# A Mamba scan: the diagonals of B are written by DMA into DRAM and loaded, in place of being built by engines

## The chip, the core and the metric

The kernel runs on one core of a Trainium2 chip. Its engines are TensorE (PE: matrix products and transposes), VectorE (DVE), ScalarE (ACT), GpSimd (POOL) and SyncE (SP, which here only issues transfers); 16 DMA engines move data between DRAM and the on-chip memory SBUF. Time is the device time of one execution in microseconds (us), from the first to the last instruction with what lies around it.

## The reference

Input x has the shape (4, 32, 32, 384). A group norm, then a visual Mamba block whose result is added to x, then another group norm and a mixture of experts, added too. The work of this case is the selective scan in the Mamba block, over sequences of L = 1024 positions, 192 channels, 16 states, for 4 directions of each of 4 images:

```
dA = exp(d_t[..., None] * As)
h  = h * dA + (d_t * u_t)[..., None] * B_t[:, :, None, :]
y  = einsum('bkcn,bkn->bkc', h, C_t)
```

d_t, B_t and C_t come from the projection x_proj. All is float32.

## The kernel before

Three parts: `head` (norm, projections, convolution; its results xd hold the rows of dt, B and C in DRAM), `scan`, and `tail` (output norm, gate, projection and experts). The change is in `scan`, and a few lines of it in `head`.

**Units and steps.** A unit is one direction of one image: 16 units, u = 0 to 15, `unit_of` gives image b, orientation o and side s. A unit has 24 steps i: 8 pairs of states n (NP), by 3 groups g of 64 channels (CG). In one step, 128 partitions hold 2 states of 64 channels, and the row has 1024 positions. Each step runs through four engines:

- PE, `spread_b` (L1002): 64 products of 64 by 64 make the input term (dt u) B in PSUM (`pb`, two buffers). A product has dt u of 64 positions by 64 channels on one side, and on the other a 64 x 64 diagonal matrix with the values of B of one state at those positions. So a position's B scales it and the product turns positions into the free dimension at the same time.
- ACT, `decay` (L1084): exp(dt A), two steps ahead.
- DVE, `step_h` (L1158): the scan itself, out of `a` and `pb` into `h`, of which there are three triples of steps (TRIPLES).
- POOL, `times_c` (L1193): h times C, twice a triple; `crow`, the row of C broadcast to the partitions, is loaded by SP (L943) with three buffers.
- PE, `add_y` (L1041): sums over states in PSUM, seven steps (LAG) behind the first.

A scan of the first step of a triple waits until `add_y` has emptied the triple of three before. `spread_b` of a step waits for the scan of two steps before, since `pb` has two buffers.

**The diagonals.** `dd`, 32 KB x 128 partitions or 4 MB, holds all of them for one unit: 16 states by 8 blocks by 64 columns; upper and lower 64 partitions hold the diagonals of positions in the two halves r of a block. It is made in four pieces of 4 states. Pieces 1 and 3 are built by POOL (`build_d`, L199), one product of a broadcast of `bt` and a mask each; pieces 0 and 2 by ACT (`build_rows`, L284), 32 small instructions each that are dealt out over 12 steps. Piece p of the next unit may be written when `spread_b` has passed step 6(p + 1) of this one (`b_row`). `bt`, B with the positions on partitions, is made by the chunk "BT": PE transposes rows of xd (L223), ACT copies them (L262).

**Chunks.** The next unit is prepared by small pieces of PE work, each put behind the two PE parts of a certain step: Z (4 chunks, steps 0 to 3), BT (step 4), UT (4 chunks, steps 5 to 8, only when the next unit is even), DUP (4 chunks, steps 16 to 19). All share one PSUM bank, `pm`, and ACT empties it after each. ACT and DVE compute the softplus between steps 4 and 15.

**The SP queue.** SP goes through the units and the pairs n in order: crow; at n = 0 the rows of the next unit (L119, L120) and in odd units u or y (L127, L133; L975 in the last); at n = 7 the doublings of dt (L209). It waits in order, so that what stands behind a wait is late too. When an image is done, y is copied out by ACT (L1089, L1090) and stored (L949, L952).

The order on each engine is that in which the code issues; nothing reorders it.

Of the kernel before, what the change touches and what calls it, by code (L numbers as in the profile page):

```python
# [11 lines left out]
P = 128  # L12
BATCH = 4
HW = 32
L = HW * HW
# [5 lines left out]
N = 16  # L21
# [27 lines left out]
LAST_U = UNITS - 1  # L49
KINDS = (2, 0, 1)  # L50
# [25 lines left out]
def chunks_of(u):  # L76

    order = [("Z", ch) for ch in range(4)] + [("BT", 0)]
    if u % 2 == 0:
        order += [("UT", ch) for ch in range(4)]  # L80
    return order + [("DUP", i) for i in range(4)]
# [33 lines left out]
def load_rows(sp, d, keep, shared, u):  # L115

    b, o, s = unit_of(u)
    rows = keep["rows"]
    sp.dma_start(rows[0:R], d["xd"][b, o, s * PR:s * PR + R]).then_inc(shared["rows_in"], 16)  # L119
    sp.dma_start(rows[PR:PR + N], d["xd"][b, o, 2 * PR + s * N:2 * PR + (s + 1) * N]).then_inc(shared["rows_in"], 16)  # L120
# [26 lines left out]
class Units:  # L147

    def __init__(self, nc, ctx, keep, ys, shared):
# [16 lines left out]
        self.bt = sb("bt", [P, 2, N, BLK])  # L166
# [23 lines left out]
        self.b_row = sem("b_row")  # L190
        self.dup_in = [sem(f"dup_in{g}") for g in range(CG)]

    def build_d(self, eng, tt, u, piece):

        eng.wait_ge(self.chunk_taken, CHUNK[u, "BT", 0] + 1)
        need(eng, self.b_row, STEPS * (u - 1) + 6 * (piece + 1) if u else 0)
        rows_n = slice(4 * piece, 4 * piece + 4)
        shape = [P, 4 * BLK, HALF]
        tt(self.dd[:, rows_n].rearrange("p n k j -> p (n k) j"),  # L199
           self.bt[:, u % 2, rows_n].rearrange("p n k -> p (n k)").unsqueeze(2).broadcast_to(shape),  # L200
           self.keep["mask"][:].unsqueeze(1).broadcast_to(shape), ALU.mult).then_inc(self.d_odd if piece % 2 else self.d_even, 1)
# [9 lines left out]
    def chunk(self, pe, u, what, i):  # L211
# [4 lines left out]
        if what == "Z":  # L216
            pe.wait_ge(self.shared["rows_in"], 16 * 2 * (u + 1))
# [23 lines left out]
    def take_chunk(self, act, u, what, i):  # L241
# [7 lines left out]
        if what == "BT":  # L249
            need(act, self.d_even, 2 * (u - 1))  # L250
            need(act, self.d_odd, 2 * (u - 1))
            dst = self.bt[:, u % 2].rearrange("p n k -> p k n")
            src = pm[:, 0:BLK * N].rearrange("p (k n) -> p k n", k=BLK)
# [23 lines left out]
    def build_rows(self, act, u, piece, lo, hi):  # L277

        if lo == 0:
            act.wait_ge(self.chunk_taken, CHUNK[u, "BT", 0] + 1)  # L280
            need(act, self.b_row, STEPS * (u - 1) + 6 * (piece + 1) if u else 0)
        for at in range(lo, min(hi, 4 * BLK)):
            n, blk = 4 * piece + at // BLK, at % BLK
            row = self.nc.scalar.activation(self.dd[:, n, blk], self.keep["mask"][:], ACT.Identity,  # L284
                                            scale=self.bt[:, u % 2, n, blk:blk + 1])
        if hi >= 4 * BLK:
            row.then_inc(self.d_even, 1)
# [111 lines left out]
def head(nc, d, keep, keep_from, ys, m, shared):  # L399
# [5 lines left out]
    with ExitStack() as ctx:  # L405
# [271 lines left out]
        def _(act):  # L677
# [112 lines left out]
            m.build_rows(act, 0, 2, 0, 2 * BLK)  # L790
# [91 lines left out]
        @block.gpsimd  # L882
        def _(pool):
            nc.gpsimd.memset(xpad[:], 0.0).then_inc(borders, 1)
            pool.wait_ge(shared["kept_in"], 16 * len(KEPT))
            pool.wait_ge(turned, NC * BATCH)
            for piece in range(2):
                m.build_d(pool, nc.gpsimd.tensor_tensor, 0, piece)


def scan(nc, d, keep, ys, m, norm, shared):

    with ExitStack() as ctx:
# [42 lines left out]
        def _(sp):  # L936
# [50 lines left out]
        def _(pe):  # L987
            def spread_b(u, i):
# [76 lines left out]
        def _(act):  # L1065
# [29 lines left out]
            for u in range(UNITS):  # L1095
                b, o, s = unit_of(u)
                for i in range(STEPS):
# [3 lines left out]
                    if u + 1 < UNITS:  # L1101
# [85 lines left out]
        def _(pool):  # L1187
# [550 lines left out]
def bass_vision_mamba_moe(nc, x, eye, win, wx, gavg, conv_p, ones, wdt, apar, dpar, mask, wout, ln_g, ln_b, wr, rb, w1, b1, w2, b2, spread, eyeb, out):  # L1738
    def scratch(name, shape, dt=F32):
# [8 lines left out]
        xd=scratch("xd", (BATCH, 2, P, L)), u=scratch("u", (PAIRS, KIND, P, L)), ub=scratch("ub", (PAIRS, 2, KIND, P, L)), y=scratch("y", (PAIRS, KIND, P, L)),  # L1748
# [111 lines left out]
```

## Time and profile before

| | us |
|---|---|
| Times of three runs | 1640.47, 1642.54, 1648.41 |
| Median | 1642.54 |
| Profiled execution | 1650.07 |
| Its span | 1648.3 |

| Engine | busy us | share |
|---|---|---|
| PE | 1349.6 | 82% |
| DVE | 1229.3 | 75% |
| POOL | 1026.4 | 62% |
| ACT | 1014.8 | 62% |

SP's queue (q1) moved 146.83 MB in 73,200 packets, 30.3% of the 16 DMA engines' time. Another 240 packets, 3.93 MB, are instructions on q8. The scan runs from 187 us or so to 1342 us, a unit in about 71 us; head and tail take the rest. Busy shares are means over parts with different limits, so a unit has to be read by itself.

### The profile page before, as it was taken

The numbers are of one execution on the slowest core, as the hardware profiler recorded it, in microseconds if no ns is written. First come the engines' busy times: TensorE is split into PE (matmuls) and PEld (weight loads), VectorE is DVE, ScalarE is ACT, GpSimd is POOL, SyncE is SP. The second block draws the span as 40 slices with busy tenths as digits, with TensorE's granted clock in tenths as the row PEclk, the third lists the DMA queues.
The fourth block names the chain that finished last, engine by engine and source line by source line (L and its number), as shares of the span: only waits on it lengthen the run. The fifth ranks groups of instructions, "written<-read, shape, count | busy, mean of one in ns | idle before, by whom it ended". The sixth has DMA issues, their size and how long they took to land. (4 is left out here: it accounts for less than half of the span.)

```text
span 1648.3 us, 66375 instructions
## 1 busy us (share of the span) xinstructions
PE 1349.6 (82%) x30408; PEld 824.1 (50%) x30408; DVE 1229.3 (75%) x1025; ACT 1014.8 (62%) x1916; POOL 1026.4 (62%) x294
## 2 busy tenths in 40 slices
PE   6997779687886979788697878869787867879998
PEld 5734546444554545455454545545454534436554
DVE  4984298979798897989889798888979884733220
ACT  2558578766777877677787767777776640402222
POOL 0002189879797988889798889979888870000000
PEclk8998689999999999999999999999999997879999
DMA  9334324323232432323343232324323325101101
GB/s 324 125 148 185 112 65 107 96 67 96 54 90 73 110 91 72 96 68 90 74 109 86 77 91 73 90 73 109 86 77 81 97 81 196 39 0 39 39 29 48
DMA packets 73478, 151.08 MB, mean 92 GB/s; under 512 B 33238, under 2 KB 41942, under 8 KB 72816
## 3 DMA queue, kind: packets, MB, share of 16 engines
q1 hardware_dynamic: 73200, 146.83, 30.3%
q8 instruction: 240, 3.93, 1.0%
q14 instruction: 38, 0.31, 0.1%
HBM read 101.72 MB, written 32.51 MB: 81 GB/s over the span
## 5 line engine op out<-in xcount | busy, mean ns | idle before, releaser
L1193 POOL TENSOR_TENSOR s_h<-s_h,s_crow 128x2048 f32<-128x2048 f32 (+1 forms) x256 | 880.2, 3469 | 198.0 <-DVE s_h L1158 197.9
L1158 DVE TENSOR_TENSOR_SCAN s_h<-s_a,s_pb 128x1024 f32<-128x1024 f32 x384 | 864.2, 2277 | 183.6 <-PE s_py L1041 78.5
L1002 PE MATMUL s_pb<-k_area,m_dtut 64*64 64x64 f32 x24576 | 470.2, 224 | 194.2 <-DVE s_h L1158 162.8
L1002 PEld LDWEIGHTS s_pb<-k_area,m_dtut 64*64 64x64 f32 x24576 | 424.1, 138 | 384.6 <-DVE s_h L1158 230.1
L1041 PE MATMUL s_py<-s_h,k_eye 64*64 64x512 f32 x3072 | 417.8, 603 | 20.4 <-ACT y_y L1090 15.6
L284 ACT ACTIVATE k_area<-k_mask,m_bt 128x64 f32<-128x64 f32 x992 | 273.9, 337 | 0.0
L1084 ACT ACTIVATE s_a<-y_y,m_aneg 128x1024 f32<-128x1024 f32 x192 | 218.6, 1139 | 39.9 <-DVE s_h L1158 39.8
L1084 ACT ACTIVATE s_a<-m_dup,m_aneg 128x1024 f32<-128x1024 f32 x192 | 219.5, 1143 | 29.7 <-DVE s_h L1158 29.7
L199 POOL TENSOR_TENSOR k_area<-m_bt,k_mask 128x2048 f32<-128x2048 f32 x33 | 145.8, 4419 | 126.1 <-ACT m_bt L262 126.1
L1041 PEld LDWEIGHTS s_py<-s_h,k_eye 64*64 64x64 f32 x3072 | 90.1, 137 | 33.3 <-ACT y_y L1090 16.0
L262 ACT COPY y_y<-m_pm 128x384 f32<-128x384 f32 (+1 forms) x96 | 49.2, 513 | 91.8 <-PE m_pm L219 79.2
L1070 ACT ACTIVATE m_pm<-y_y 128x512 f32<-128x512 f32 x45 | 26.8, 596 | 98.5 <-DVE y_y L1141 98.5
L219 PEld LDWEIGHTS m_pm<-k_wdt,k_rows 25*128 25x128 f32 x256 | 42.4, 196 | 56.9 <-issue 56.5
L1473 PE MATMUL t_small<-k_w,k_area 128*128 128x384 f32 x192 | 70.4, 504 | 0.0
L1538 ACT COPY t_out<-t_small 128x384 f32<-128x384 f32 x32 | 15.3, 479 | 88.4 <-PE t_small L1476 88.4
L1448 PE MATMUL t_big<-t_xn,k_w 128*128 128x512 f32 x144 | 67.9, 623 | 0.0
L219 PE MATMUL m_pm<-k_wdt,k_rows 25*128 25x192 f32 x256 | 62.5, 366 | 6.5 <-DMA k_rows<-scratch_xd 6.5
L805 DVE SCALAR_TENSOR_TENSOR h_acc<-h_xpad,h_conv_p,h_acc 128x1024 f32<-128x1024 f32 x48 | 61.7, 1285 | 1.6
L238 PEld LDWEIGHTS m_pm<-k_eye,y_y 64*64 64x64 f32 (+1 forms) x512 | 33.6, 123 | 52.9 <-issue 49.9
L1659 DVE TENSOR_TENSOR k_area<-k_area,t_big 128x1024 f32<-128x1024 f32 x12 | 14.3, 1219 | 50.6 <-PE t_big L1462 50.4
L1473 PEld LDWEIGHTS t_small<-k_w,k_area 128*128 128x128 f32 x192 | 37.0, 197 | 18.5 <-issue 1.9
L238 PE MATMUL m_pm<-k_eye,y_y 64*64 64x64 f32 (+1 forms) x512 | 42.9, 224 | 2.7 <-ACT y_y L262 2.7
(189 smaller groups left out, 1233.5 us busy)
## 6 DMA issues: line engine op xcount, KB each, us to landing
s_crow<-scratch_xd SPq DMA_DIRECT2D x256, 256.0 KB, 4.0
k_area<-in_x_dram SPq DMA_DIRECT2D x4, 1536.0 KB, 8.0
scratch_xt<-y_y SPq DMA_DIRECT2D x4, 1536.0 KB, 10.2
y_y<-y_y SPq DMA_DIRECT2D x24, 256.0 KB, 3.6
m_dup<-m_dup SPq DMA_DIRECT2D x24, 256.0 KB, 3.2
out_dram<-t_out SPq DMA_DIRECT2D x32, 192.0 KB, 1.9
k_area<-scratch_xt SPq DMA_DIRECT2D x3, 1536.0 KB, 6.9
scratch_xd<-h_dbl SPq DMA_DIRECT2D x8, 512.0 KB, 2.6
```

Of the source, the lines that this page charges most:

```text
L199: tt(self.dd[:, rows_n].rearrange("p n k j -> p (n k) j"), self.bt[:, u % 2, rows_n].rearrange("p n k -> p (n k)").unsqueeze(2).broadcast_ ...
L219: mm = pe.matmul(pm[:, x * DI:(x + 1) * DI], tokens(rows[0:R + 1], 2 * i + x), self.keep["wdt"][:, o + 2 * s], start=True, stop=True)
L238: mm = pe.transpose(pm[0:chans.stop - chans.start, blk::BLK], self.dt_of[here, blk, chans], eye[here, here])
L284: row = self.nc.scalar.activation(self.dd[:, n, blk], self.keep["mask"][:], ACT.Identity, scale=self.bt[:, u % 2, n, blk:blk + 1])
L805: eng.scalar_tensor_tensor(out, view, w, out, ALU.mult, ALU.add).then_inc(convolved[kind], 1)
L1002: mm = pe.matmul(pb[par * HALF:(par + 1) * HALF, step % 2, r * BANK + blk:(r + 1) * BANK:BLK], dtut[here, u % 2, blk, g * HALF:(g + 1) * H ...
L1041: mm = pe.matmul(dst, eye[here, here], src, start=opens, stop=closes)
L1084: nc.scalar.activation(a[:, step % RING], dup[u % 2][:, g], ACT.Exp, scale=aneg[:, col:col + 1]).then_inc(a_ready, 1)
L1158: nc.vector.tensor_tensor_scan(h[:, step % (TRIPLES * CG), f], a[:, step % RING, f], pb[:, step % 2, f], 0.0, ALU.mult, ALU.add).then_inc( ...
L1193: nc.gpsimd.tensor_tensor(here, here, c.unsqueeze(1).broadcast_to([P, groups.stop - groups.start, L]), ALU.mult).then_inc(hc_ready, 1)
L1448: mm = pe.matmul(big_of("F1", b, j)[:, q], w1[:, c, j * P:(j + 1) * P], xn[:, b % 2, c, q], start=(c == 0), stop=(c == NC - 1))
L1473: pe.matmul(ps, hid[:, j, tok], w2[:, j], start=False, stop=False, skip_group_check=True)
```

## The change

From unit 1 on no engine builds diagonals. A scratch tensor `dd` in DRAM, four pieces of 128 x 2048 floats, gets the diagonals of unit 0 by `store_d`, zeros included. For each later unit `write_diagonal` overwrites the 64 places of each diagonal, straight from the rows of B in xd, also in DRAM: two DMAs a piece, one for each half r, with 32 diagonals of 64 elements; neighbours in the destination lie 2,049 elements apart. `load_d` then brings the piece, 1 MB, into SBUF. All on SP's queue: for unit u + 1 the writes of pieces 0 to 2 at n = 2, 4, 6 and the loads at n = 3, 5, 7; piece 3 at n = 0 and 1 of its own unit. PE waits for the load's semaphore (`d_in`).

The chunk BT, the load of its rows, and `build_d` and `build_rows` stay for unit 0 alone; `bt` has one buffer. The rows of the next unit wait for its chunk Z 3 in place of BT.

The core of the diff:

```diff
-    order = [("Z", ch) for ch in range(4)] + [("BT", 0)]
+    order = [("Z", ch) for ch in range(4)]
+    if u == 0:
+        order += [("BT", 0)]
...
+    def write_diagonal(self, sp, d, u, piece):
+
+        b, o, s = unit_of(u)
+        sp.wait_ge(self.d_stored[piece] if u == 1 else self.d_in[piece], 16 * max(u - 1, 1))
+        there = d["dd"][piece]
+        first = 2 * PR + s * N + 4 * piece
+        rows = d["xd"][b, o, first:first + 4].rearrange("n (k r j) -> r (n k) j", r=2, k=BLK)
+        for r in range(2):
+            diagonal = bass.AP(tensor=there.tensor, offset=there.offset + r * HALF * QUARTER, ap=[[HALF, 4 * BLK], [QUARTER + 1, HALF]])
+            sp.dma_start(diagonal, rows[r], allow_slow_non_contiguous=True).then_inc(self.d_written[piece], 16)
+
+    def load_d(self, sp, d, u, piece):
+
+        sp.wait_ge(self.d_written[piece], 32 * u)
+        sp.wait_ge(self.b_row, STEPS * (u - 1) + 6 * (piece + 1))
+        sp.dma_start(self.quarter(piece), d["dd"][piece]).then_inc(self.d_in[piece], 16)
+
+    def store_d(self, sp, d, piece):
+
+        sp.wait_ge(self.d_odd if piece % 2 else self.d_even, piece // 2 + 1)
+        sp.dma_start(d["dd"][piece], self.quarter(piece)).then_inc(self.d_stored[piece], 16)
...
                     if n == 0 and u + 1 < UNITS:
-                        sp.wait_ge(chunk_done, CHUNK[u, "BT", 0] + 1)
+                        sp.wait_ge(chunk_done, CHUNK[u, "Z", 3] + 1)
                         load_rows(sp, d, keep, shared, u + 1)
...
+                    if u == 0 and n < 4:
+                        m.store_d(sp, d, n)
+                    if n in (2, 4, 6) and u + 1 < UNITS:
+                        m.write_diagonal(sp, d, u + 1, (n - 2) // 2)
+                    if n in (3, 5, 7) and u + 1 < UNITS:
+                        m.load_d(sp, d, u + 1, (n - 3) // 2)
+                    if n == 0 and u:
+                        m.write_diagonal(sp, d, u, 3)
+                    if n == 1 and u:
+                        m.load_d(sp, d, u, 3)
...
-                    pe.wait_ge(d_odd if piece % 2 else d_even, 2 * u + piece // 2 + 1)
+                    if u == 0:
+                        pe.wait_ge(d_odd if piece % 2 else d_even, piece // 2 + 1)
+                    else:
+                        pe.wait_ge(m.d_in[piece], 16 * u)
...
-                        if 6 <= i < 18:
-                            m.build_rows(act, u + 1, 0, share(i - 6), share(i - 5))
-                        if i >= 18:
-                            m.build_rows(act, u + 1, 2, share(i - 18), share(i - 17))
-                    if i < 6:
-                        m.build_rows(act, u, 2, share(i + 6), share(i + 7))
+                    if u == 0 and i < 6:
+                        m.build_rows(act, 2, share(i + 6), share(i + 7))
...
-                    if n == 1:
-                        m.build_d(pool, nc.gpsimd.tensor_tensor, u, 3)
-                    if n == 4 and u + 1 < UNITS:
-                        m.build_d(pool, nc.gpsimd.tensor_tensor, u + 1, 1)
+                    if u == 0 and n == 1:
+                        m.build_d(pool, nc.gpsimd.tensor_tensor, 3)
```

## Rows read from the trace of the kernel before

**Rows 1.** Waits, whole run: engine, line, releaser; us in total, times, longest.

```profile
DVE s_h L1158 <- PE s_py L1041: 78.5, 72, 4.6
...
DVE s_h L1158 <- PE s_pb L1002: 63.2, 43, 6.1
...
PE s_pb L1002 <- issue: 25.4, 31, 3.6
...
PE s_py L1041 <- ACT y_y L1090: 15.6, 3, 5.2
```

**Rows 2.** Groups by line: count, busy us, mean ns; idle before, releasers.

```profile
L1041 PE MATMUL s_py<-s_h,k_eye 64*64 64x512 f32 x3072 | 417.8, 603 | 20.4 <-ACT y_y L1090 15.6 <-POOL s_h L1193 2.3 <-issue 1.2
L284 ACT ACTIVATE k_area<-k_mask,m_bt 128x64 f32<-128x64 f32 x992 | 273.9, 337 | 0.0
...
L199 POOL TENSOR_TENSOR k_area<-m_bt,k_mask 128x2048 f32<-128x2048 f32 x33 | 145.8, 4419 | 126.1 <-ACT m_bt L262 126.1
```

**Rows 3.** Windows: thirds of one unit; busy us (instructions), clock, DMA share, GB/s.

```profile
556.00:581.00 25.00, 25.00 (x706) 16.96 (x706) 20.18 (x9) 21.55 (x43) 23.09 (x8) 1.00 0.29 77
581.00:605.00 24.00, 15.65 (x536) 8.89 (x528) 22.54 (x19) 15.06 (x32) 18.80 (x6) 1.00 0.29 80
605.00:627.00 22.00, 19.00 (x603) 12.32 (x604) 20.43 (x11) 17.17 (x36) 22.00 (x7) 1.00 0.40 109
```

**Rows 4.** Timeline around BT: start us, us, what; in brackets idle before.

```profile
567.25 0.67 PE L223 MATMUL m_pm<-k_eye,k_rows 16*128 16x16 f32 x8
...
567.85 1.16 PE L1002 MATMUL s_pb<-k_area,m_dtut 64*64 64x64 f32 x64
...
570.90 1.16 PE L1002 MATMUL s_pb<-k_area,m_dtut 64*64 64x64 f32 x64
...
573.09 4.46 DVE L1158 TENSOR_TENSOR_SCAN s_h<-s_a,s_pb 128x1024 f32<-128x1024 f32 x2 [1.73 <-PE s_py L1041]
```

**Rows 5.** Timeline of DVE in a unit without UT, steps 3 to 6.

```profile
781.33 6.67 DVE L1158 TENSOR_TENSOR_SCAN s_h<-s_a,s_pb 128x1024 f32<-128x1024 f32 x3 [1.47 <-PE s_py L1041]
788.46 4.47 DVE L1158 TENSOR_TENSOR_SCAN s_h<-s_a,s_pb 128x1024 f32<-128x1024 f32 x2 [0.46 <-PE s_py L1041]
```

**Rows 6.** Timeline where ACT takes y away.

```profile
499.96 0.81 ACT L284 ACTIVATE k_area<-k_mask,m_bt 128x64 f32<-128x64 f32 x3
...
503.08 0.57 ACT L284 ACTIVATE k_area<-k_mask,m_bt 128x64 f32<-128x64 f32 x2
...
505.08 1.88 PE L1041 MATMUL s_py<-s_h,k_eye 64*64 64x512 f32 x8 [5.19 <-ACT y_y L1090]
```

**Rows 7.** DMA in 507.6:508.9, 1276:1279 and 546:617: packets, or queue with share.

```profile
DMA packets 1683, 0.13 MB, mean 98 GB/s; under 512 B 1678, under 2 KB 1678, under 8 KB 1683
...
DMA packets 240, 0.96 MB, mean 321 GB/s; under 512 B 5, under 2 KB 5, under 8 KB 240
...
q1 hardware_dynamic: 3076, 6.65, 34.2%
```

**Rows 8.** DMA in 401:406 and 406:407; PE's timeline at three stops.

```profile
q1 hardware_dynamic: 483, 1.24, 90.2%
...
DMA packets 875, 0.23 MB, mean 233 GB/s; under 512 B 874, under 2 KB 874, under 8 KB 874
...
q8 instruction: 1, 0.02, 7.5%
...
408.75 0.62 PE L1002 MATMUL s_pb<-k_area,m_dtut 64*64 64x64 f32 x26 [2.68 <-issue]
...
701.10 0.74 PE L1002 MATMUL s_pb<-k_area,m_dtut 64*64 64x64 f32 x34 [1.89 <-issue]
...
1282.33 0.97 PE L1002 MATMUL s_pb<-k_area,m_dtut 64*64 64x64 f32 x50 [3.58 <-issue]
```

**Rows 9.** DMA issues (KB, us to landing), then SP's timeline.

```profile
scratch_y<-y_y SPq DMA_DIRECT2D x8, 128.0 KB, 6.1
...
546.88 1.10 SPq L943 DMA_DIRECT2D s_crow<-scratch_xd  x2
```

More of the change, by code:

```diff
@@ L49 @@
 LAST_U = UNITS - 1
+QUARTER = 4 * BLK * HALF
 KINDS = (2, 0, 1)
@@ L119, in load_rows @@
     sp.dma_start(rows[0:R], d["xd"][b, o, s * PR:s * PR + R]).then_inc(shared["rows_in"], 16)
-    sp.dma_start(rows[PR:PR + N], d["xd"][b, o, 2 * PR + s * N:2 * PR + (s + 1) * N]).then_inc(shared["rows_in"], 16)
+    if u == 0:
+        sp.dma_start(rows[PR:PR + N], d["xd"][b, o, 2 * PR + s * N:2 * PR + (s + 1) * N]).then_inc(shared["rows_in"], 16)
 def load_u(sp, d, keep, shared, b, what):
@@ L165, in __init__ @@
         self.dtut = sb("dtut", [P, 2, BLK, DI])
-        self.bt = sb("bt", [P, 2, N, BLK])
+        self.bt = sb("bt", [P, N, BLK])
         self.amin = sb("amin", [P, UNITS // BATCH * STEPS])
@@ L190, in __init__, with build_d @@
         self.b_row = sem("b_row")
+        self.d_in = [sem(f"d_in{piece}") for piece in range(4)]
+        self.d_stored = [sem(f"d_stored{piece}") for piece in range(4)]
+        self.d_written = [sem(f"d_written{piece}") for piece in range(4)]
         self.dup_in = [sem(f"dup_in{g}") for g in range(CG)]
-    def build_d(self, eng, tt, u, piece):
-        eng.wait_ge(self.chunk_taken, CHUNK[u, "BT", 0] + 1)
-        need(eng, self.b_row, STEPS * (u - 1) + 6 * (piece + 1) if u else 0)
+    def build_d(self, eng, tt, piece):
+        eng.wait_ge(self.chunk_taken, CHUNK[0, "BT", 0] + 1)
         rows_n = slice(4 * piece, 4 * piece + 4)
@@ L199, in build_d @@
         tt(self.dd[:, rows_n].rearrange("p n k j -> p (n k) j"),
-           self.bt[:, u % 2, rows_n].rearrange("p n k -> p (n k)").unsqueeze(2).broadcast_to(shape),
+           self.bt[:, rows_n].rearrange("p n k -> p (n k)").unsqueeze(2).broadcast_to(shape),
            self.keep["mask"][:].unsqueeze(1).broadcast_to(shape), ALU.mult).then_inc(self.d_odd if piece % 2 else self.d_even, 1)
@@ L216, in chunk @@
         if what == "Z":
-            pe.wait_ge(self.shared["rows_in"], 16 * 2 * (u + 1))
+            pe.wait_ge(self.shared["rows_in"], 16 * (u + 2))
             for x in range(2):
@@ L249, in take_chunk @@
         if what == "BT":
-            need(act, self.d_even, 2 * (u - 1))
-            need(act, self.d_odd, 2 * (u - 1))
-            dst = self.bt[:, u % 2].rearrange("p n k -> p k n")
+            dst = self.bt[:].rearrange("p n k -> p k n")
             src = pm[:, 0:BLK * N].rearrange("p (k n) -> p k n", k=BLK)
@@ L275, in exponent, with quarter, build_rows @@
             nc.scalar.activation(self.wz, ez, ACT.Identity, bias=1.0).then_inc(self.w_ready, 1)
-    def build_rows(self, act, u, piece, lo, hi):
+    def write_diagonal(self, sp, d, u, piece):
[14 more added lines that the diff above has]
+        sp.dma_start(d["dd"][piece], self.quarter(piece)).then_inc(self.d_stored[piece], 16)
+    def quarter(self, piece):
+        return self.keep["area"][:].rearrange("p a l -> p (a l)")[:, piece * QUARTER:(piece + 1) * QUARTER]
+    def build_rows(self, act, piece, lo, hi):
         if lo == 0:
-            act.wait_ge(self.chunk_taken, CHUNK[u, "BT", 0] + 1)
-            need(act, self.b_row, STEPS * (u - 1) + 6 * (piece + 1) if u else 0)
+            act.wait_ge(self.chunk_taken, CHUNK[0, "BT", 0] + 1)
         for at in range(lo, min(hi, 4 * BLK)):
@@ L284, in build_rows @@
             row = self.nc.scalar.activation(self.dd[:, n, blk], self.keep["mask"][:], ACT.Identity,
-                                            scale=self.bt[:, u % 2, n, blk:blk + 1])
+                                            scale=self.bt[:, n, blk:blk + 1])
         if hi >= 4 * BLK:
@@ L789, in _ @@
             act.wait_ge(turned, NC * BATCH)
-            m.build_rows(act, 0, 2, 0, 2 * BLK)
+            m.build_rows(act, 2, 0, 2 * BLK)
         def convolve(eng, pair, kind, taps=range(9)):
@@ L887, in _ @@
             for piece in range(2):
-                m.build_d(pool, nc.gpsimd.tensor_tensor, 0, piece)
+                m.build_d(pool, nc.gpsimd.tensor_tensor, piece)
 def scan(nc, d, keep, ys, m, norm, shared):
@@ L995, in spread_b @@
                     piece = i // 6
-                    pe.wait_ge(d_odd if piece % 2 else d_even, 2 * u + piece // 2 + 1)
+                    if u == 0:
+                        pe.wait_ge(d_odd if piece % 2 else d_even, piece // 2 + 1)
+                    else:
+                        pe.wait_ge(m.d_in[piece], 16 * u)
                 need(pe, h_ready, step - 1)
@@ L1747, in bass_vision_mamba_moe @@
         xt=scratch("xt", (BATCH, NC, P, L)), sz=scratch("sz", (PAIRS, P, TT, 2 * DI)),
-        xd=scratch("xd", (BATCH, 2, P, L)), u=scratch("u", (PAIRS, KIND, P, L)), ub=scratch("ub", (PAIRS, 2, KIND, P, L)), y=scratch("y", (PAIRS, KIND, P, L)),
+        dd=scratch("dd", (4, P, QUARTER)), xd=scratch("xd", (BATCH, 2, P, L)), u=scratch("u", (PAIRS, KIND, P, L)), ub=scratch("ub", (PAIRS, 2, KIND, P, L)), y=scratch("y", (PAIRS, KIND, P, L)),
     )
```

## The prediction

> **What bounds the kernel now.** I read the waits of the whole run first [rows 1]. VectorE (DVE), which carries the scans, waited for TensorE (PE) on both of its PE lines, 78.5 us for L1041 and 63.2 us for L1002. GpSimd (POOL) and ScalarE (ACT) are next, and the groups by line [rows 2] close that question for POOL: PE's idle time before L1041, the only line that reads what POOL multiplies, holds 15.6 us for ACT and 2.3 us for POOL. So POOL ends nobody's wait, and ACT those 15.6 us. The same view prices what the change takes away: 992 rows of L284 (273.9 us of ACT) and 33 products of L199 (145.8 us of POOL).
>
> Then I cut one unit in three [rows 3]. In its first 25 us, steps 0 to 8, PE is busy for all 25.00 us and DVE for 20.18: PE binds. In the next 24 us PE is busy for 15.65 and DVE for 22.54: DVE binds (scans and the softplus). In the last 22 us both stand near: 19.00 and 20.43. In no third does ACT or POOL bind. A gain must come from PE in the first third; a loss, too, comes at once from whatever stops PE there.
>
> **What the change takes off the path.** Of the 31 products and 960 rows that go from the scan, the engines' time off the critical path is worth nothing: POOL is hidden behind LAG, seven steps, and ACT runs two steps ahead. If that cover were gone POOL's 4.4 us would show as a PE wait for POOL, and there are 2.3 us of those in all. Two things do lie on the path.
>
> (A) The chunk "BT" goes for 15 units: eight PE transposes between two steps. In a unit that also turns u [rows 4], L1002 starts at 567.85, right behind BT's transposes, and again at 570.90: a step with a UT chunk is 3.05 us of PE without a gap. The first scan of the next three starts 2.19 us behind L1002 (573.09 after 570.90), having waited 1.73 us for PE. BT's transposes take 0.67 us (L223). The whole stretch is PE's, so 0.67 us goes whole. There are 7 such units: 4.7 us. In the other 8 there is no UT chunk; scans start at 781.33 and 788.46 [rows 5], 7.13 us for three, and three scans alone are 6.67: DVE becomes the bound after about 0.5 us. 8 x 0.5 = 4.0. Sum 8.7 us; between 0 (if something else holds the step) and 15 x 0.67 = 10.
>
> (B) ACT copies y away in three units (L1089, L1090), and PE waits for it: 15.6 us in three waits [rows 1]. At the one at 505 us [rows 6] ACT's rows show no idle time in front of the copies, and blocks of L284 stand among its work: 0.81 us at 499.96, 0.57 right ahead of the copies, and a third like the first a step earlier. Without them ACT is 2.2 us earlier, and so is PE. 3 x 2.2 = 6.6 us, between 0 and 8.
>
> **What it adds: transfers.** All on SP's queue and the 16 DMA engines. Per unit: 8 writes of 32 x 64 single 4-byte elements, the address step between neighbours 8,196 bytes, so 16,384 packets; 4 loads of 1 MB; minus one 64 KB load of rows. Once, in unit 0: 4 stores of 1 MB.
> Price of an element: no row shows a 4-byte packet into DRAM. The nearest one is the store of y2, runs of 64 bytes into DRAM: 1683 packets in 1.3 us [rows 7], so 2,048 take 1.6 us and a unit's 16,384 take 12.7 us. The packets of 256 bytes (874 in 1 us, [rows 8]) would make it 18.7. I take 12.7, as the store goes the same way and is short too.
> Price of a load: 0.96 MB in 3 us in a long load from DRAM [rows 7], so 3.3 us for a piece and 13 us a unit.
> The unit has 71 us, of which the DMA engines were busy for 34.2% [rows 7], or 24 us. With 12.7 and 13 it is 50 of 71 us: no saturation.
>
> Waits on SP. The write at n waits for a load of one unit ago. The load at n + 1 waits for that write, issued one group (a unit's 71 us by 8, about 9) earlier, which needs 3.2 us for the two halves, or 6.1 to landing as y2 has it [rows 9]. Its wait for b_row asks PE for a step or two more than SP has waited POOL for, so a us or two. What stands behind it on SP: the next crow, the doubling at n = 7 and the rows of the next unit. Crow has three buffers and is issued two groups (17 us) before use; the doublings wait for ACT anyway. Every piece is loaded three groups or more before its first step. I cost all these at nothing; if a write took more than 20 us, crow would be late.
> The 4 MB stored in unit 0 I cost at nothing too, bounded by 0 and 13 us.
>
> (C) What the bursts do to PE. PE's instructions are themselves fetched by DMA: the page has 240 instruction packets on q8 (3.93 MB, 16 KB each) and PE 60,816 instructions, so a packet brings about 253, under two steps. The DMA answer by stretch counts them. From 401 to 406 us, while SP's transfers of a unit start (crow, rows, u: 1.24 MB, share 90.2%), there is no q8 packet at all; the next is in 406 to 407, and PE resumes at 408.75 after 2.68 us of "issue", idle with no semaphore to blame [rows 8]. The same at 1282.33 (3.58 us, behind the 1.5 MB load of y) and at 701.10 (1.89). That a late instruction packet is the cause is my inference. Eight units start with such a long burst, and three of them stop PE: (2.68 + 3.58 + 1.89) / 8 = 1.0 us each. Bursts of crow alone do not (0.52 MB a group; at the unit's 24 us for 6.65 MB [rows 7], 1.9 us): PE is at 25.00 of 25 us through them.
> The change makes every group's burst long: crow 1.9 + two writes 3.2 = 5.1 us at n = 2, 4, 6, crow + load 3.3 = 5.2 us at n = 3, 5, 7 and 1, and with the rows, and u in every second unit, 5.6 to over 8 us at n = 0. The long ones of before moved 1.24 MB in 5 us and went on to 407. SP runs ahead: n = 0 is issued at 546.88 [rows 9], for a unit whose first third starts at 556 [rows 3]. So, a group being 9 us, n = 2 and 3 fall in the first third (some 560 to 575), 7, 0 and 1 in the last third of the unit before, n = 4 on the seam, and 5 and 6 in the middle third, where PE has 8 us to spare. I count the five as four whole ones, since the last third has 3 us to spare, each at 0.75 us, as they are a little shorter than those priced at 1.0. 15 units x 4 x 0.75 = 45 us. Ends: 0, if the packets of q8 slip in between; 15 x 7 = 105, if nearly half of the five stop PE by the mean stop of 2.7 us, which a first third without slack allows.
>
> A rule of the Trainium skill stands against (C): "Runtime: NRT & Kernel Launch", section "Instruction fetch mechanics", says that the sequencer fetches the next 16 KiB page while it runs the present one, and that crossing a page costs one tail bump, mostly hidden. By that rule (C) is nought and the sum is -15.3 us, about 1627. The trace agrees on the size of the packets and differs on hidden at three places, 8.15 us in all.
>
> **Sum.** The profiled execution took 1650.07 us (span 1648.3, 1.8 around it). 1650.1 - 8.7 - 6.6 + 45 = 1679.8. The median of the runs shown is 7.5 below the profiled one, so 1672.
>
> **Rivals.**
> 1. Transfers stay hidden (faster). PE's instruction packets get in between SP's; then only (A) and (B) count: 1642.5 - 15.3 = 1627. For it: the crow bursts, 8 a unit, leave PE full; the share stays at 70%; five of eight long bursts stopped nothing visible. Against: the new ones stand 8 to a unit, and where PE has no slack.
> 2. Element writes are slow and DMA fills up (much slower). Place: the queue of SP's rings. 24 + 13 us of other work leave 34 us of a unit for 8 writes, so from 4.3 us a write (2.7 times the price of y2's) the DMA engines bind, loads wait for writes on SP, crow comes late and POOL stops. At 5.5 us a write: (37 + 44 - 71) x 15 = 150 us more, less the gain, 1777. For it: the address step of 8 KB, that the source is DRAM too, and no row with 4 bytes. Against: the 64-byte and 256-byte packets differ by less than a factor of two, so a packet costs a fixed time.
> 3. (C) is about as large as (A) + (B): small stops of 1 us a unit, within the bound, 1642. It needs the coincidence.
> That the change doesn't do what it says: the zeros are never overwritten and the elements are the same values; the first unit still builds its own. I give that nothing.
>
> **Chances.** Forecast (stops of 25 to 105 us in sum) 0.52; rival 1 0.28; rival 2 0.12; rival 3 0.08. 0.5% (8.2 us) is about what a measurement of this kernel can tell from no change. Faster 0.28, within it 0.08, slower 0.64. The range goes from rival 1 with a little to spare, 1624, to beyond the upper end of (C) (1642.5 - 15.3 + 105 = 1732), part way into rival 2: 1745. The forecast's own range is 1652 to 1732.
>
> **What would show it.** (A): in the first third, three steps 0.67 us (0.5 without UT) shorter from one first-of-three scan to the next. (B): the wait of PE for L1090's successor down from 5.2 to about 3 us, three times. (C): PE's idle time under "issue" on L1002 up from 25.4 us to some 60 or more [rows 1], in gaps of 1 to 4 us behind stretches of DMA share 0.9, and the units' first thirds longer than 25 us. POOL and ACT 130 and 260 us less busy with no effect on DVE's waits besides. Packets up by 245,760, DMA share in a unit near 70%; landing of the element writes near 6 us (over 10 speaks for rival 2). The forecast is wrong if PE's issue idle stays at 25 us.

## The result, and the profile after

| | before | after |
|---|---|---|
| Median of four runs, us | 1641.94 | 1759.37 |
| Lowest and highest | 1640.47, 1648.41 | 1748.92, 1773.32 |
| Span of the profiled execution | 1648.3 | 1747.1 |
| Mean granted TensorE clock in it | 0.942 | 0.918 |

The changed kernel takes 1.0699 of the time before, 95% interval 1.0639 to 1.0759: 7% slower. Forecast were 1672 and a range that ends at 1745. Some executions of a kernel take over 1.5% more than its fastest; medians, ratios and intervals here leave them out. The execution of after that was traced is the fastest of its four, so the profiles show 98.8 us of a loss of 117.

The page of after: share of PE's clock and of the DMA engines in 40 slices, the queues, groups by line (busy us, mean ns, idle before), and the landing time of the loads, issue by issue.

```profile
span 1747.1 us, 65285 instructions
PE 1393.7 (80%) x30288; PEld 855.8 (49%) x30288; DVE 1235.5 (71%) x1025; ACT 792.1 (45%) x941; POOL 895.8 (51%) x264
...
PEclk8998688999999899989898989999999997989999
DMA  9324566555656656465665546566564634200101
...
q1 hardware_dynamic: 329616, 213.95, 48.5%
q8 instruction: 239, 3.92, 1.0%
...
L1044 PE MATMUL s_pb<-k_area,m_dtut 64*64 64x64 f32 x24576 | 502.9, 229 | 241.4 <-DVE s_h L1196 118.5
...
L1083 PE MATMUL s_py<-s_h,k_eye 64*64 64x512 f32 x3072 | 458.0, 637 | 26.4 <-issue 16.5
...
s_crow<-scratch_xd SPq DMA_DIRECT2D x256, 256.0 KB, 4.7
k_area<-scratch_dd SPq DMA_DIRECT2D x60, 1024.0 KB, 6.6
```

ACT and POOL are relieved as planned: busy 792 and 896 us, where the table of before has 1015 and 1026. By itself that buys little, since POOL ended next to none of PE's waits and ACT 15.6 us of them [rows 1]. DVE is busy as before (1235.5 against 1229.3), so all that is new lies in its waits, and those that grew name PE (its waits for ACT are 41.8 us, 38.9 before):

```profile
DVE s_h L1196 <- PE s_pb L1044: 121.5, 77, 6.1
...
DVE s_h L1196 <- PE s_py L1083: 117.9, 73, 5.1
PE s_pb L1044 <- issue: 116.9, 75, 5.4
...
PE s_py L1083 <- issue: 16.5, 13, 2.8
```

239.4 us, where [rows 1] have 141.7: plus 97.7, and the span grew by 98.8. PE in turn stands still under "issue", with no semaphore to blame: 116.9 us in 75 stops, 25.4 in 31 before, and 16.5 us ahead of L1083, 1.2 before [rows 2]. PE's wait for ACT's copies of y, 15.6 us in [rows 1], is down to 1.9 us.

The three thirds of one unit, as in [rows 3]. The columns are the stretch and its length, the busy us of PE, of its weight loads (PEld), of DVE, ACT and POOL with their instructions in brackets, then PE's granted clock, the DMA share and GB/s.

```profile
593.00:621.00 28.00, 26.02 (x632) 17.30 (x629) 19.36 (x9) 15.86 (x18) 17.13 (x6) 0.91 0.62 152
621.00:645.00 24.00, 16.91 (x526) 11.40 (x529) 21.10 (x18) 10.19 (x12) 15.62 (x5) 0.86 0.53 124
645.00:671.00 26.00, 20.67 (x679) 13.15 (x670) 22.48 (x12) 13.11 (x15) 18.84 (x7) 1.00 0.62 136
```

78 us for 71. The DMA share has about doubled in the first two thirds. The clock column shows a second thing: in the first two thirds PE was granted 0.91 and 0.86, where before it had 1.00 throughout.

**What follows a stop.** Two views at one place, the seam between two units: PE's timeline, then the windows around it.

```profile
759.47 0.38 PE L1044 MATMUL s_pb<-k_area,m_dtut 64*64 64x64 f32 x3 [3.17 <-issue]
...
763.16 1.99 PE L1044 MATMUL s_pb<-k_area,m_dtut 64*64 64x64 f32 x64
764.92 1.93 PE L1083 MATMUL s_py<-s_h,k_eye 64*64 64x512 f32 x8
```

```profile
758.00:760.00 2.00, 0.54 (x9) 0.51 (x13) 0.00 (x1) 0.00 (x0) 2.00 (x1) 0.59 1.05 342
760.00:762.00 2.00, 2.00 (x9) 0.42 (x2) 2.00 (x1) 0.00 (x0) 0.83 (x1) 0.50 0.99 178
762.00:764.00 2.00, 2.00 (x36) 1.56 (x39) 0.28 (x1) 0.74 (x2) 1.57 (x1) 0.50 0.58 58
764.00:766.00 2.00, 2.00 (x52) 1.17 (x44) 0.00 (x0) 0.79 (x1) 0.79 (x1) 0.50 0.27 2
```

PE stood still for 3.17 us while the DMA share was about 1; then its clock is granted at 0.50, the level of 1.2 GHz, for the rest of the stretch, and the same 64 products take 1.99 us that take 1.16 in [rows 4]. Not every stop has this behind it: after 2.23 us at 507.46 and after 0.85 us at 603.64 the clock stays at 1.00. Summed over windows of 2 us from 188 us to the end of the scan, the share of full clock that is missing comes to 94 us, against 37.5 before; at two levels that is 188 and 75 us spent at 1.2 GHz. It shows in the groups too: L1044 and L1083 are busy for 72.9 us more, for the same products (502.9 + 458.0 against 470.2 + 417.8).

**What ends a stop.** The DMA engines in the 6 us ahead of the stop of 3.17 us (750 to 756), then in the microsecond in which it begins (756 to 757):

```profile
q1 hardware_dynamic: 2282, 0.50, 61.3%
```

```profile
q1 hardware_dynamic: 38, 0.17, 88.6%
q8 instruction: 1, 0.02, 7.7%
```

No instruction packet (q8) comes for 6 us; then one comes, and PE resumes at 759.47. It is so at every stop. Taken microsecond by microsecond, the scan of before has 227 such packets and 33 stops of PE under "issue", that of after 224 and 89. Each stop has a packet of its own and ends 2.2 to 3.9 us behind the start of the microsecond in which that packet appears; of arbitrary moments only a third lie so behind one. So the stops are waits for instructions.

**What the transfers do.** The 1 us in which a pair of element writes begins (601 to 602), and the 4 us behind it: all packets, then SP's queue.

```profile
DMA packets 1592, 0.07 MB, mean 68 GB/s; under 512 B 1580, under 2 KB 1580, under 8 KB 1591
...
DMA packets 2358, 0.01 MB, mean 2 GB/s; under 512 B 2358, under 2 KB 2358, under 8 KB 2358
...
q1 hardware_dynamic: 2358, 0.01, 28.2%
```

Elements start at 1,592 in 1 us and go on at 2,358 in 4 us, 590 a us, on engines that count as busy for 28%. A pair of writes (4,096) takes about 5 us, where I had assumed 3.2.

### The profile page after: what moved, and what is told of

Its sections match the earlier page's. It is cut to its first block and busy times, and to the rows that moved or that the text cites. A ratio compares the mean times of both kernels' runs of the same rounds, so it can differ in the third digit from the quotient of the medians.

```text
span 1747.1 us, 65285 instructions
## 1 busy us (share of the span) xinstructions
PE 1393.7 (80%) x30288; PEld 855.8 (49%) x30288; DVE 1235.5 (71%) x1025; ACT 792.1 (45%) x941; POOL 895.8 (51%) x264
## 5 line engine op out<-in xcount | busy, mean ns | idle before, releaser
L1044 PE MATMUL s_pb<-k_area,m_dtut 64*64 64x64 f32 x24576 | 502.9, 229 | 241.4 <-DVE s_h L1196 118.5
L1044 PEld LDWEIGHTS s_pb<-k_area,m_dtut 64*64 64x64 f32 x24576 | 457.1, 143 | 437.6 <-issue 259.0
L1083 PE MATMUL s_py<-s_h,k_eye 64*64 64x512 f32 x3072 | 458.0, 637 | 26.4 <-issue 16.5
L1083 PEld LDWEIGHTS s_py<-s_h,k_eye 64*64 64x64 f32 x3072 | 101.5, 143 | 48.0 <-issue 32.5
L205 POOL TENSOR_TENSOR k_area<-m_bt,k_mask 128x2048 f32<-128x2048 f32 x3 | 13.7, 4576 | 126.4 <-ACT m_bt L266 126.4
L225 PEld LDWEIGHTS m_pm<-k_wdt,k_rows 25*128 25x128 f32 x256 | 46.2, 211 | 64.8 <-issue 64.5
L225 PE MATMUL m_pm<-k_wdt,k_rows 25*128 25x192 f32 x256 | 67.8, 390 | 5.9 <-DMA k_rows<-scratch_xd 5.8
L1574 ACT COPY t_out<-t_small 128x384 f32<-128x384 f32 x32 | 15.3, 479 | 86.0 <-PE t_small L1512 86.0
L1484 PEld LDWEIGHTS t_big<-t_xn,k_w 128*128 128x128 f32 x144 | 27.0, 194 | 32.5 <-issue 31.6
```

What stands on the lines that cost most here:

```text
L1044: mm = pe.matmul(pb[par * HALF:(par + 1) * HALF, step % 2, r * BANK + blk:(r + 1) * BANK:BLK], dtut[here, u % 2, blk, g * HALF:(g + 1) * H ...
L1083: mm = pe.matmul(dst, eye[here, here], src, start=opens, stop=closes)
L1484: mm = pe.matmul(big_of("F1", b, j)[:, q], w1[:, c, j * P:(j + 1) * P], xn[:, b % 2, c, q], start=(c == 0), stop=(c == NC - 1))
```

## The experiments

Two theories were carried into them. **X**: long bursts of data hold back PE's instruction packets, and PE stops. **Y**: something else of the change makes the time, such as the slow element writes and what queues behind them on SP, or the waits that PE and SP gained. Kernels without loads use unit 0's diagonals throughout, and kernels without writes load unit 0's again, so B of the later units is left out of both; "above e1" is the ratio to the kernel before, less e1's. Ratios compare with runs of the kernel before from the same session, in which it took 1647 to 1654 us, 5 to 12 more than beside the change.

**Which part costs.** Where the loads go (e1, e3), PE's wait for `d_in` goes with them; waits of SP for a transfer that no longer comes are replaced by one for the stores of unit 0.

```diff
e1_neither, e3_writes_only
-                        m.load_d(...)
...
-                        pe.wait_ge(m.d_in[piece], 16 * u)
...
e1_neither, e2_loads_only
-                        m.write_diagonal(...)
...
e2_loads_only
-        sp.wait_ge(self.d_written[piece], 32 * u)
+        sp.wait_ge(self.d_stored[piece], 16)
...
```

> The kernel after without the writes and loads of diagonals from unit 1 on (every unit uses those of unit 0, so B of the later units is left out); the stores of unit 0 stay. It prices terms (A) and (B) alone. My theory (late instruction packets behind SP's bursts cost the time): 15 us less than before, about 1627, PE's issue idle on L1044 back near 25 us from 116.9. Rival (leaving out BT and the rows itself costs something, by another order of PE's work or a lower clock): 1642 or more.

> As after, but the element writes from unit 1 on are left out, while the 60 loads of 1 MB stay (they bring the diagonals of unit 0). My theory, bursts count by their length whatever is in them: the loads are 3.3 us of each 5.2 us burst in every other group, about half of the loss, 1627 + 60 = 1687 (1665 to 1710). Rival (small packets are what hurts): within 10 us of the run without either, under 1640.

> As after, but the loads of 1 MB are left out and the element writes stay (the products use the diagonals of unit 0). My theory: the other half, 1627 + 60 = 1687 (1665 to 1710). Rival (small packets are what hurts): nearly all of the loss, 1740 or more. If both runs stay under 1660, it is only the sum of the two that fills the queue.

The last two columns are PE's "issue" stops ahead of its two scan lines, and the time at 1.2 GHz in the scan, from windows of 2 us.

| | median us | ratio [95%] | above e1 | span | stops us | at 1.2 GHz |
|---|---|---|---|---|---|---|
| before | 1651.84 | 1 | | 1648.3 | 26.6 | 75 |
| e1 | 1628.93 | 0.9852 [0.9808, 0.9896] | 0 | 1629.6 | 31.4 | 77 |
| e2 | 1698.89 | 1.0282 [1.0201, 1.0363] | 0.043 | 1689.4 | 80.5 | 110 |
| e3 | 1713.87 | 1.0386 [1.0326, 1.0446] | 0.053 | 1707.0 | 84.0 | 143 |
| after | 1759.37 | 1.0699 [1.0639, 1.0759] | 0.085 | 1747.1 | 133.4 | 188 |

Without the transfers the change is a gain of 1.5%; the transfers cost 8.5%. Either part alone costs half of that or more, and both together cost less than the sum of the two (0.096). e2's four times scatter most, from 1691 to 1733 us, and its row rests on the lower two; the mean of all four would give 1.038, the size of e3. From e1 to after, span, stops and time at the low clock rise together; before and e1 are alike in both. In e1, which differs from after only in its transfers and the wait for them, PE's stops and DVE's waits are back at the level of [rows 1]:

```profile
DVE s_h L1196 <- PE s_py L1083: 74.4, 66, 4.7
...
DVE s_h L1196 <- PE s_pb L1044: 55.1, 40, 6.0
...
PE s_pb L1044 <- issue: 25.5, 23, 2.9
```

Here too the stops end behind a packet of q8: all 31 of e1 and all 67 of e2 by 2.3 to 4.0 us, 65 of e3's 71 by 2.0 to 3.9.

**Other places and other pieces.** If a burst costs only where PE has no slack, the middle third should take them for nothing.

```diff
e4_spread: half a write and half a load behind every step of PE
+            sp.wait_ge(self.b_row, at + r)
e5_writes_middle: writes at n = 5, 6, for the units ahead; loads unchanged
e6_writes_first: writes at n = 2, 3
-                    if n in (2, 4, 6) and u + 1 < UNITS:
+                    if n in (2, 3) and u + 1 < UNITS:
+                        m.write_diagonal(sp, d, u + 1, 2 * n - 4)
+                        m.write_diagonal(sp, d, u + 1, 2 * n - 3)
e7_all_middle: all loads and writes at n = 4, 5, 6
```

> The whole of after, the same bytes and packets, but each write (of one half r) and each half of a load waits for one more step of PE (b_row), so that a group's burst of 5 us is cut into pieces of 1.6 to 1.9 us a step apart. My theory (a stop comes when an instruction packet waits behind several us of queued transfers): most of the loss goes, 1660 (1635 to 1690), PE's issue idle under 60 us. Rival (the traffic itself slows PE, DVE or SBUF, or the lower clock does it, wherever it stands): no change from 1759, within 15 us.

> All of after's transfers, the loads where they were; the element writes of a unit (12.7 us of DMA work) are moved from n = 0, 2, 4, 6 to n = 5 and 6, the middle third of a unit, where DVE binds and PE takes its instructions more slowly. e4 refuted that it is the length of a burst that counts. New theory: an instruction packet is late whenever it meets SP's traffic, and that costs time only in the thirds where PE binds. Then the writes' part nearly goes, 1715 (1695 to 1730), near e2_loads_only. Rival (amount alone counts, or contention of writes with everything): 1759, within 12 us.

> The opposite of e5: all the element writes of a unit at n = 2 and 3, in or just ahead of the first third. New theory: as many writes as after has in exposed places (three of four pieces) or more, 1760 to 1790. Rival (amount alone): 1759, within 12 us. If it is below 1740, the place of the third is not what decides.

> Loads and writes both moved to n = 4, 5 and 6, 32 us of DMA work with crow in some 28 us. New theory: most of both parts goes, 1665 (1640 to 1700). Rival (a full DMA queue there holds up crow or an instruction packet by more than DVE's slack of 1.7 us a step): 1720 or more, with PE stops in the middle third or POOL waiting for crow.

Measured: e4 1.0977 [1.0924, 1.1030], e5 1.1303 [1.1251, 1.1354], e6 1.0928 [1.0880, 1.0977], e7 1.1033 [1.0964, 1.1102] (1813, 1862, 1801 and 1820 us). All are slower than the change itself. In none of the four did the theory's time come. In e4, e5 and e6 the rival's did not come either; e7 fits its rival, with POOL waiting 42.3 us for crow. e4 speaks against the word "long" in X: the same bytes in pieces a step apart stop PE for more (169.5 us on the two lines), not less. In e5 the waits name what comes late besides PE's instructions:

```profile
PE s_pb L1046 <- issue: 146.0, 70, 5.2
...
ACT s_a L1128 <- DMA m_dup<-m_dup: 101.3, 9, 31.8
ACT s_a L1128 <- DMA y_y<-y_y: 84.2, 7, 15.9
...
PE m_pm L225 <- DMA k_rows<-scratch_xd: 45.1, 9, 24.4
...
POOL s_h L1233 <- DMA s_crow<-scratch_xd: 28.9, 5, 12.8
```

ACT waits for the doublings, PE for the rows, POOL for crow: all that stands behind the writes on SP. And the elements are slow there too; all packets in 11 us of e5, 674 to 685:

```profile
DMA packets 6700, 0.07 MB, mean 6 GB/s; under 512 B 6696, under 2 KB 6696, under 8 KB 6696
...
q1 hardware_dynamic: 6699, 0.05, 34.2%
```

That is 610 a us. To see each part by itself in the middle:

```diff
f1_writes_middle_alone: e5 without the loads
f2_loads_middle_alone: e7 without the writes
```

> The element writes of e5 at n = 5 and 6, with no loads of diagonals from unit 1 on (the products use those of unit 0). e3, the same writes at n = 0, 2, 4, 6, took 1714, and 1629 is the time without transfers. Theory (a transfer costs where PE binds; e5 failed since slow writes and the loads behind them ran over into the last third and held doublings and rows): 1660 (1645 to 1685), PE's issue idle under 50 us. Rival (slow writes in one lump cost as much or more wherever they stand): 1714 or more.

> The loads of e7 at n = 4, 5 and 6, with no element writes from unit 1 on. e2, the same loads at n = 1, 3, 5, 7, took 1715. Theory (place decides for the loads): 1650 (1640 to 1675). Rival (amount decides): 1700 or more.

f1 is 1.0462 [1.0384, 1.0540], f2 1.0039 [1.0004, 1.0073] (1720 and 1653 us): for f1 the rival held, for f2 the theory. For loads the place decides: above e1, 0.043 where the change has them (e2) and 0.019 in the middle, where part of what is left is a load that PE had to wait for (19.2 us in three waits). For the writes it does not (0.053 and 0.061). SP's timeline in f1:

```profile
691.33 11.89 SPq L291 DMA_DIRECT2D scratch_dd<-scratch_xd  x4
703.27 2.41 SPq L973 DMA_DIRECT2D s_crow<-scratch_xd  x2
705.78 11.03 SPq L291 DMA_DIRECT2D scratch_dd<-scratch_xd  x4
```

Four writes keep SP for 11 to 12 us, two such lumps for a whole third, and the middle third does not hold them.

**Size of a load.**

```diff
f6_half_loads: e2, each load 512 KB instead of 1 MB
-        sp.dma_start(self.quarter(piece), d["dd"][piece])
+        sp.dma_start(self.quarter(piece)[:, 0:QUARTER // 2], d["dd"][piece][:, 0:QUARTER // 2])
```

> As e2_loads_only (same 60 loads at n = 1, 3, 5, 7, no element writes), but each brings 512 KB in place of 1 MB, so a group's burst is 3.5 us and not 5.2. By ratios to before, no transfers is 0.985 and whole loads 1.028. Theory (a burst costs by what of it is longer than PE's store of instructions lasts): more than half of the cost goes, ratio 0.995 (0.987 to 1.003). Rival (each byte costs alike): half, ratio 1.007. Rival 2 (each DMA costs alike, whatever its size): ratio 1.02 or more.

0.9970 [0.9931, 1.0008], 1646 us, with 61.1 us of stops on the two lines and 82 us at 1.2 GHz. Above e1, 0.012 for half the bytes, 0.043 for all: the cost grows faster than the bytes of a load (half of 0.043 lies just outside the intervals). Whether that is the length of the burst or the amount, f6 can't tell, since it halves both.

**Why the writes are slow.**

```diff
e10_writes_step65: e3, neighbours 65 elements apart in DRAM
-... ap=[[HALF, 4 * BLK], [QUARTER + 1, HALF]]
+... ap=[[HALF * HALF, 4 * BLK], [HALF + 1, HALF]]
e11_act_queue: after, the writes issued by ACT on its own queue, at eight steps
-            sp.dma_start(diagonal, rows[r], ...)
+        act.dma_start(diagonal, rows[r], ...)
f3_from_sbuf: e3, the elements come from a constant in SBUF
-            sp.dma_start(diagonal, rows[r], ...)
+            sp.dma_start(diagonal, self.keep["mask"][0:4 * BLK], ...)
f4_rows_in_sbuf: after, the rows of B first loaded to SBUF (64 KB a unit) and written from there
f5_rows_in_sbuf_middle: the same on e7
```

> As e3_writes_only (loads left out, products use the diagonals of unit 0), but the elements of a diagonal go 65 elements (260 bytes) apart in DRAM in place of 2,049 (8,196 bytes): same count, same bytes, another layout that nobody reads. In after, the packets of a write run at some 600 a us behind the first 2,000 or so, in e8_mixed those of element loads into SBUF at 1,500. Theory: single elements into DRAM are slow as such: rate near 600, time within 15 us of e3 (1714). Rival: the step of 8 KB makes them slow (few banks or pages): rate near 1,300 or more and time under 1680.

> After whole, but the element writes are issued by ACT on its own DMA queue, at steps that answer to SP's places (1, 2, 8, 9, 14, 15, 22, 23); the loads stay on SP. Theory X: a slow write holds up what stands behind it in SP's queue (crow, doublings, rows, loads), and that is much of the loss: 1710 (1690 to 1730), landing of crow back from 4.7 to about 4 us and of the doublings from 6.9 to under 5. Theory Y: the 16 engines under it are what is held, whatever queue issues, PE's instruction packets too: 1759 within 15 us, with PE's issue idle near 117 us. If ACT's own issue time hurts, ACT's decay comes late and DVE waits for ACT.

> As e3_writes_only, places and counts the same, but the elements come from SBUF (a constant tile; the values written are not B) in place of DRAM. Theory (it is the write into DRAM that is slow): the packets behind the first 2,000 run at 600 a us again and the time is that of e3, 1714 within 15 us. Rival (DRAM on both sides makes it slow): a rate over 1,000 and under 1690 us.

> After whole and in the same places, but the 16 rows of B of a unit are first loaded into SBUF (64 KB, 128 runs of 512 bytes, one DMA at n = 0) and the element writes take them from there, so no single element is read from DRAM and written to DRAM by one packet. f3 lowered the writes' part from 85 to 46 us that way. Theory (slow element copies from DRAM to DRAM hold the DMA engines): 1720 (1700 to 1735), rate of the packets near 1,200 a us. Rival (with the loads there the writes' pace does not matter): 1759 within 10 us.

> e7 (loads and writes at n = 4, 5 and 6) with the rows of B in SBUF as in f4. e7 took 1823 with the slow writes, f2 with its loads alone 1654. Theory (place decides as long as the transfers there end before the last third): 1690 (1660 to 1715), no long waits of ACT for the doublings (138 us in e7). Rival (writes cost more in a lump, fast or slow): 1740 or more.

e10 is 1.0419 [1.0367, 1.0470], no better than e3, and its packets run at 500, 534 and 455 in the three us from 597 on: the address step is not it. e11 is 1.0875 [1.0816, 1.0935], 1790 us and more than either theory had: another queue doesn't spare PE. f3 is 1.0176 [1.0116, 1.0237], as its rival had it, above e1 0.032 where e3 has 0.053. Landing times of the same 120 writes, in e10 and in f3, and the packets of a stretch of 4 us in f3:

```profile
scratch_dd<-scratch_xd SPq DMA_DIRECT2D x120, 8.0 KB, 8.2
```

```profile
scratch_dd<-k_mask SPq DMA_DIRECT2D x120, 8.0 KB, 6.4
...
DMA packets 3895, 0.06 MB, mean 16 GB/s; under 512 B 3887, under 2 KB 3887, under 8 KB 3893
...
q1 hardware_dynamic: 3893, 0.04, 52.6%
```

Single elements copied from DRAM to DRAM are the slow form; out of SBUF they are 3,895 in 4 us, at least 970 a us. But mending that hardly helps the change: f4 is 1.0624 [1.0558, 1.0691], 1751 us where I expected 1720, and its interval overlaps that of after. f5 is 1.0758 [1.0704, 1.0812], 42 us below e7 and no better than after. Both fit their rivals. So the writes' pace is a part of e3's cost, but as long as the 1 MB loads are there PE's stops stay: 99.8 us in f4 on the first line.

**The gains by themselves, on the kernel before.**

```diff
e9_y_first: in three units ACT copies y ahead of its rows
+                    early = s == 0 and o == 0 and u > 0
+                    if i == 6 and early:
+                        take_y(b - 1)
+                        m.build_rows(act, u, 2, share(10), share(12))
-                    if i < 6:
+                    if i < (4 if early else 6):
e8_mixed: e9, and from unit 2 on bt is loaded as single elements at n = 5, 6
+    sp.dma_start(self.bt[:, u % 2, ...], d["xd"][...].rearrange("n (k p) -> p n k", p=P))
e12_bt_seam: e8 with these loads at n = 7 and 0
-                    if n in (5, 6) and u + 2 < UNITS:
+                    if n == 7 and u + 2 < UNITS: ...
+                    if n == 0 and 0 < u < UNITS - 1: ...
```

> The kernel before with one edit: in the three units where an image's y is taken away, ACT copies it before it builds the rows of that and the last step. Theory of term (B): ACT's rows hold PE up there by 2.2 us, three times: 6 to 7 us less, ratio 0.996 (0.993 to 0.999). Rival: PE then waits for something else and nothing changes, ratio 1.000.

> The kernel before with two edits: from unit 2 on bt is loaded by DMA element by element at n = 5 and 6 two units ahead (16,384 elements of 4 bytes read from DRAM, no PE transposes, no ACT copy; the engines still build the diagonals); and where y is taken away ACT does that before it builds rows. New theory: both gains (A) 8 us and (B) 7 us, and little for transfers in the middle third: 1629 against 1642 of before, ratio 0.992 (0.985 to 0.998). Rival (element transfers cost wherever they stand, as in e3: 85 us): ratio 1.02 or more.

> As e8_mixed, but the element loads of bt stand at n = 7 and n = 0, around the seam of two units where PE has little slack, in place of n = 5 and 6. If the place of a transfer matters for such loads, which do not last longer than their packets say: 1655 to 1675 against 1638 of e8. If it does not: within 8 us of e8.

e9 is 0.9934 [0.9904, 0.9964], e8 0.9937 [0.9905, 0.9969], e12 1.0123 [1.0073, 1.0172] (1639, 1638 and 1669 us). PE's wait for ACT in e9, 15.6 us in [rows 1]:

```profile
PE s_py L1041 <- ACT y_y L1090: 5.8, 3, 1.9
```

e8 also saves the BT chunks of 14 units and ends where e9 does. Either that frees little or its 16,384 element reads a unit take it back; no run tells which. They run fast, 8,349 packets in the 9 us of e8 from 661 to 670, and 1,423, 1,386 and 1,560 in the three us from 666 on:

```profile
DMA packets 8349, 0.56 MB, mean 62 GB/s; under 512 B 8227, under 2 KB 8227, under 8 KB 8347
...
q1 hardware_dynamic: 8347, 0.52, 71.0%
```

Moved to the seam (e12) the same reads cost 31 us, and the stops on `pb`'s line go from 33.9 to 54.4 us. e9 and e8 are the versions that beat both kernels.

## Why the prediction was right and wrong

**What binds: right.** POOL and ACT gave up 131 and 223 us of work (forecast 130 and 260), and the waits of DVE that grew name only PE. A slip without weight: 30 products of `build_d` go and not 31, since three of the 33 stay (L205).

**(A) and (B): right in kind, priced somewhat low.** They were to bring 15.3 us, 0.9%. e1, which has them and not the transfers, gained 1.5% [1.0, 1.9], 23 us against the 1652 of its own session; that its 1629 stands beside the forecast 1627 is luck, since the kernel before was 10 us slower there. For (B) alone I had 6.6 with 8 at most; in e9 the wait fell by 9.8 us and the time by 0.7%, some 11 us. (A) by itself was not measured without transfers; e1 less e9 leaves 0.8% for it and all the rest.

**(C): right in kind, mis-sized.** This is the step that failed: "four whole ones, each at 0.75 us", 45 us for 15 units. Measured: 0.085 by ratio, 139 us (1759.4 - 1628.9 = 130 across two sessions). The 0.75 us was a mean over bursts most of which stop nothing: three stops over eight long bursts of before. The stops on the two lines went from 33 to 88, 55 more or 3.7 a unit, nearly one for each of the four bursts, and 106.8 us over 55 stops is 1.9 us each: 7.1 us a unit for my 3. That is the upper end I had given (105 us), so the stops alone stay near the range. Why so many more bursts stop PE is not shown; f6 against e2 says only that the cost runs ahead of the bytes. And the stop is only the first half of the price: I put the clock at nothing. It was there to be read in the kernel before; these are its windows behind the stop that ends at 408.75 in [rows 8]:

```profile
408.00:410.00 2.00, 1.25 (x35) 0.66 (x35) 0.00 (x0) 0.00 (x0) 2.00 (x1) 0.92 0.88 244
410.00:412.00 2.00, 2.00 (x8) 1.13 (x4) 1.09 (x1) 0.00 (x0) 2.00 (x2) 0.50 0.04 10
412.00:414.00 2.00, 2.00 (x66) 1.73 (x68) 1.20 (x1) 1.62 (x4) 1.25 (x1) 0.50 0.00 0
414.00:416.00 2.00, 2.00 (x21) 0.39 (x13) 1.67 (x1) 0.39 (x1) 0.00 (x0) 0.50 0.76 209
```

Some 6 us at 1.2 GHz behind 2.68 us of standing: about 3 us of PE's work more. In the whole run the stops grew by 107 us and PE's work on its two lines by 73; of these 180 us, DVE's waits took over 98, and that is net of what (A) and (B) gained; the rest fell where PE has slack.

That a late instruction packet makes the stops was my inference, and the traces bear it out: each of the 122 stops in the scans of before and after ends behind the arrival of a packet of its own. Data traffic alone brings more of them, also where PE waits for no transfer that was added (e3), and taking it away removes them (e1). No run slowed or sped the packets of q8 alone, so how the traffic delays them stays open.

The rule of the skill that I set against (C), that crossing a page of instructions is mostly hidden (the Trainium skill, "Runtime: NRT & Kernel Launch", section "Instruction fetch mechanics"), holds for the greater part of the packets and not for the rest: 89 of the 224 in the scan of after end a stop, 33 of 227 before, and 133 us of PE's time stand under "issue".

**The price of an element write: wrong, and of little weight.** "2,048 take 1.6 us" came from stores out of SBUF in runs of 64 bytes; from DRAM to DRAM the steady pace is near 600 a us. This is rival 2's mechanism, at 2.5 us a write instead of its 4.3: the DMA engines did not fill up (0.62 in a unit's first third, near 0.59 over the unit where I had 0.70), POOL waited for crow once, for 0.6 us, and curing it gave some 10 us (f4), within the uncertainty. It shows only where writes are put in lumps (e5, f1).

**Waits on SP and the doublings at nothing: held** as the change places them; ACT's waits for `m_dup` and `y_y` are not among the long ones of after (1.0 us in all), though SP itself waited 90.0 us for the writes. They hold by a thin margin: one step more of spread (e4), and ACT waits for both:

```profile
ACT s_a L1130 <- DMA m_dup<-m_dup: 28.4, 9, 6.5
...
ACT s_a L1130 <- DMA y_y<-y_y: 23.5, 7, 4.2
```

**Left open.** Why stops rise to 146 to 153 us on `pb`'s line alone in e4, e5 and e6, with the same bytes; and how the share of each single burst in the loss is made up, since the parts are not additive.

## What to carry to other kernels

Where one engine runs a long unrolled stream and binds, transfers are not free even at half load: look at its "issue" stops, at what the DMA engines did just before, and at the granted clock behind them, and price a stop with both. Price work that is taken away by the waits it ends and not by its busy time: 354 us of POOL and ACT were worth 1.5% here (e1), and the transfers in their place cost 8.5%. Move fewer bytes (f6); cutting the same bytes into pieces did not help (e4). Loads cost less where the binding engine has slack (f2), as long as nothing that is needed soon stands behind them (e5). Price a transfer by a row with the same source, destination and element size, or take its bounds much wider.

## What the runs showed of the hardware that I had not expected

- Each stop of PE under "issue" in the scans of before and after (33 and 89) ended 2.2 to 3.9 us behind the start of the microsecond in which an instruction packet appeared.
- Single 4-byte elements: some 600 a us from DRAM to DRAM (590 in after, 610 in e5), at least 970 out of SBUF into DRAM (f3), 914 from DRAM into SBUF in the mean of e8's 9 us and 1,386 to 1,560 in three of them. A step of 260 bytes in place of 8,196 made it no faster (e10, 455 to 534).
- A stream of such copies from DRAM to DRAM counts as 28 to 34% busy (after, e5) while SP stays behind it for 11 to 12 us a lump (f1): the DMA share doesn't show that a queue is held up.
- A stop of PE of 2.68 us was followed by 6 us at 1.2 GHz (before, 410 to 416), one of 3.17 us by over 10 (after, 760 to 772), one of 2.23 us (after, 507) and one of 0.85 us (after, 603) by none.
- Loads of 512 KB cost 1.2% above e1 and loads of 1 MB 4.3%, with the same number of them.
- Traffic issued on ACT's queue stops PE as that on SP's does (126.9 us of stops on `pb`'s line in e11, 116.9 in after).
